# Loads and stores of a per-sample matrix product carry two tiles each instead of one

## The chip, the core and the metric

The kernel runs on one core of a Trainium2 chip; the other cores are idle. The metric is the device time of one launch in microseconds (us). The inputs and the output lie in the chip's memory (HBM), and each of the core's 16 DMA engines moves a share of every transfer between HBM and the on-chip memory (SBUF).

## What is computed

Each of 128 samples has a matrix x of 128 channels by 1024 times, and a subject number from 0 to 7 that picks one of eight 128x128 weight matrices. The product is added to x:

```python
w = weights[subjects]                       # 128 x 128 x 128, picked by subject
out = jnp.einsum('bct,bcd->bdt', x, w)      # per sample
x = x + out                                 # fp32, 128 x 128 x 1024
```

64 MiB (67.1 MB) are read and as many are written, all fp32.

## The kernel before

**Tiles.** One tile is two samples, 1 MiB: 128 partitions with 8 KB each, where the partition holds two neighbouring channels of one sample, side by side. The first 64 partitions are the first sample and the other 64 the second. In HBM a tile is one contiguous 1 MiB. There are 64 tiles, worked in 8 turns of 8. x_ring holds 8 tiles of input, out_ring 8 tiles of output, one slot for each tile of a turn, 64 KB per partition each. Each slot has a semaphore of its own for its load (`x_loaded[s]`) and one for its store (`stored[s]`); a transfer raises its semaphore by 16, one by each DMA engine.

**Set-up.** SyncE's queue issues the load of the weights (0.5 MB, line 71) and then the loads of tiles 0 to 7 (line 73). TensorE (line 123) and VectorE (line 153) build a table in which each weight matrix already contains the identity, so that the addition of x comes with the product. GpSimd (line 112) copies the chosen matrix of each sample from the table to `selected`, four tiles ahead at most.

**Per tile.** TensorE (lines 130 to 145) waits for the tile's load, for its selected weights, and for the PSUM buffer of two tiles earlier, and runs 16 matmuls of 64x512 into `products` (two PSUM buffers); it then counts up `product_ready`. VectorE (line 168) and ScalarE (line 189) each copy half of the products to the tile's slot in out_ring, after `stored[s]` has shown that the slot's store of a turn earlier has landed. ScalarE then waits for both halves and issues the tile's store (line 195).

**Loads of later turns.** SyncE's queue does nothing but this: it waits until `product_ready` shows that tile k is multiplied, and issues the load of tile k + 8 into the same slot (line 80). The loads and the stores therefore form two streams, one issued by SyncE and one by ScalarE, and both are carried out by the same 16 DMA engines.

Of the kernel before, what the change touches and what calls it, by code (L numbers as in the profile page):

```python
# [7 lines left out]
I32 = mybir.dt.int32  # L8

TILES_PER_TURN = 8  # L10
PSUM_BUFS = 2
SELECT_BUFS = 4
BANK = 512
DMA = 16
HALF = 64

DRAINED_FREE = 2 * PSUM_BUFS
PRODUCT_FREE = SELECT_BUFS


def subject_mix_kernel(nc: bass.Bass, x: bass.AP, subjects: bass.AP, weights: bass.AP, out: bass.AP):
    samples, channels, times = x.shape
    n_subjects, _, mixed = weights.shape
    row = 2 * times
    tiles = samples // 2
    turns = tiles // TILES_PER_TURN
    banks = times // BANK
    wide = 2 * mixed
    flat = n_subjects * mixed
    assert channels == mixed == 2 * HALF and banks * BANK == times and flat == times  # L30
    assert turns * TILES_PER_TURN == tiles and TILES_PER_TURN % SELECT_BUFS == 0


    x_rows = x.rearrange("b (q e) t -> (b q) (e t)", e=2)
    out_rows = out.rearrange("b (q e) t -> (b q) (e t)", e=2)

    with ExitStack() as ctx:  # L37
        def sem(name):
            return ctx.enter_context(nc.semaphore(name))

        x_ring = ctx.enter_context(nc.sbuf_tensor("x_ring", [channels, TILES_PER_TURN, row], F32))
        out_ring = ctx.enter_context(nc.sbuf_tensor("out_ring", [channels, TILES_PER_TURN, row], F32))
        loaded = ctx.enter_context(nc.sbuf_tensor("loaded", [channels, n_subjects, mixed], F32))
# [6 lines left out]
        subject_row = ctx.enter_context(nc.sbuf_tensor("subject_row", [1, samples], I32))  # L50
        products = ctx.enter_context(nc.psum_tensor("products", [mixed, PSUM_BUFS, 2, times], F32))

# [5 lines left out]
        weights_spread = sem("weights_spread")  # L58
        table_ready = sem("table_ready")
        weights_selected = sem("weights_selected")  # L60
        x_loaded = [sem(f"x_loaded{s}") for s in range(TILES_PER_TURN)]
        stored = [sem(f"stored{s}") for s in range(TILES_PER_TURN)]
        product_ready = sem("product_ready")
        even_drained = sem("even_drained")
        odd_drained = sem("odd_drained")
# [3 lines left out]
        @block.sync  # L69
        def _(sp):  # L70
            sp.dma_start(loaded[:], weights.rearrange("n c d -> c n d")).then_inc(weights_loaded, DMA)
            for s in range(TILES_PER_TURN):
                sp.dma_start(x_ring[:, s], x_rows[s * channels:(s + 1) * channels, :]).then_inc(x_loaded[s], DMA)

            with sp.Fori(0, turns - 1) as turn:
                for s in range(TILES_PER_TURN):
                    tile = turn * TILES_PER_TURN + s

                    sp.wait_ge(product_ready, PRODUCT_FREE + tile + 1)
                    sp.dma_start(x_ring[:, s], x_rows[bass.ds((tile + TILES_PER_TURN) * channels, channels), :]  # L80
                                 ).then_inc(x_loaded[s], DMA)

        @block.gpsimd
        def _(pool):
# [30 lines left out]
        @block.tensor  # L115
        def _(pe):
            pe.sem_inc(product_ready, PRODUCT_FREE)
            pe.wait_ge(spread_ready, 1)
            pe.wait_ge(weights_loaded, DMA)
            for e in range(2):  # L120
                for n in range(banks):
                    cols = slice(n * BANK, (n + 1) * BANK)
                    last = nc.tensor.matmul(products[:, 0, e, cols], spread[:, e * channels:(e + 1) * channels],  # L123
                                            loaded[:].rearrange("c n d -> c (n d)")[:, cols], start=True, stop=True)
                last.then_inc(weights_spread, 1)

            with pe.Fori(0, turns) as turn:
                for s in range(TILES_PER_TURN):
                    tile = turn * TILES_PER_TURN + s
                    k, b = s % SELECT_BUFS, s % PSUM_BUFS  # L130
                    pe.wait_ge(x_loaded[s], turn * DMA + DMA)
                    pe.wait_ge(weights_selected, 2 * tile + 2)

                    pe.wait_ge(even_drained, DRAINED_FREE + 2 * (tile - PSUM_BUFS) + 2)
                    pe.wait_ge(odd_drained, DRAINED_FREE + 2 * (tile - PSUM_BUFS) + 2)
                    for n in range(banks):
                        for e in range(2):
                            for g in range(2):
                                part = slice(g * HALF, (g + 1) * HALF)
                                last = nc.tensor.matmul(  # L140
                                    products[:, b, g, n * BANK:(n + 1) * BANK],
                                    selected[part, k, e * mixed:(e + 1) * mixed],
                                    x_ring[part, s, e * times + n * BANK:e * times + (n + 1) * BANK],
                                    start=(e == 0), stop=(e == 1))
                    last.then_inc(product_ready, 1)

        @block.vector
        def _(dve):
            dve.sem_inc(even_drained, DRAINED_FREE)
            dve.wait_ge(unit_ready, 2)  # L150
            for e in range(2):
                dve.wait_ge(weights_spread, e + 1)  # L152
                nc.vector.tensor_tensor(  # L153
                    table[:, :, e * mixed:(e + 1) * mixed].rearrange("p n (b m) -> p n m b", b=2),
                    products[:, 0, e, :].rearrange("p (n m b) -> p n m b", n=n_subjects, b=2),
                    unit[:, e * mixed:(e + 1) * mixed].rearrange("p (m b) -> p m b", b=2).unsqueeze(1).to_broadcast(
                        [channels, n_subjects, HALF, 2]),
                    ALU.add).then_inc(table_ready, 1)

            def go_round(turn, first=False):  # L160
                for s in range(TILES_PER_TURN):
                    tile = turn * TILES_PER_TURN + s
                    dve.wait_ge(product_ready, PRODUCT_FREE + tile + 1)
                    if not first:

                        dve.wait_ge(stored[s], turn * DMA)
                    for b in range(2):
                        nc.vector.tensor_copy(out_ring[0:HALF, s, b * times:(b + 1) * times],  # L168
                                              products[b * HALF:(b + 1) * HALF, s % PSUM_BUFS, 0, :]
                                              ).then_inc(even_drained, 1)  # L170

            go_round(0, first=True)
            with dve.Fori(1, turns) as turn:  # L173
                go_round(turn)

        @block.scalar
        def _(act):
            act.dma_start(subject_row[:], subjects.rearrange("(a b) -> a b", a=1)).then_inc(subjects_loaded, DMA)
            act.sem_inc(odd_drained, DRAINED_FREE)

            def go_round(turn, first=False):
                for s in range(TILES_PER_TURN):
                    tile = turn * TILES_PER_TURN + s
                    act.wait_ge(product_ready, PRODUCT_FREE + tile + 1)
                    if not first:

                        act.wait_ge(stored[s], turn * DMA)  # L187
                    for b in range(2):
                        nc.scalar.copy(out_ring[HALF:channels, s, b * times:(b + 1) * times],  # L189
                                       products[b * HALF:(b + 1) * HALF, s % PSUM_BUFS, 1, :]  # L190
                                       ).then_inc(odd_drained, 1)

                    act.wait_ge(odd_drained, DRAINED_FREE + 2 * tile + 2)
                    act.wait_ge(even_drained, DRAINED_FREE + 2 * tile + 2)
                    act.dma_start(out_rows[bass.ds(tile * channels, channels), :],
                                  out_ring[:, s]).then_inc(stored[s], DMA)

            go_round(0, first=True)
            with act.Fori(1, turns) as turn:
                go_round(turn)  # L200
            for s in range(TILES_PER_TURN):
                act.wait_ge(stored[s], turns * DMA)


# [14 lines left out]
```

## Time and profile before

| | us |
|---|---|
| time, median of 3 runs | 327.03 |
| lowest and highest of the 3 | 325.48, 327.35 |
| time of the profiled execution | 326.79 |
| span of that execution, first to last instruction | 324.8 |
| TensorE busy | 239.8 (74%) |
| VectorE busy | 160.2 (49%) |
| ScalarE busy | 130.0 (40%) |
| GpSimd busy | 52.7 (16%) |

The profiled execution stands 0.24 us under the median, and its span 2.0 us under its own time. A DMA is issued by an instruction of a queue (SPq is SyncE's, ACTq is ScalarE's) that lasts a third to half of a microsecond; the movement itself goes on afterwards and is seen in the DMA share, in GB/s, and in the time from issue to landing. The releaser that the profile names for a wait is inferred: where the named engine was done already, it was another, often a DMA.

### The profile page before, as it was taken

To read this page: it belongs to the slowest core of one execution; us is meant where nothing else is said; L and a number is where in the kernel's file an instruction comes from. 1 tells how busy PE (TensorE), PEld (TensorE's weight loads), DVE (VectorE), ACT (ScalarE), POOL (GpSimd) and SP (SyncE) were. 2 spreads that over 40 slices of the span, in tenths; PEclk is the share of its full clock that TensorE was granted. 3 is DMA by queue.
4 is the path that set the end of the run, shared out by engine and by line. 5 is a ranking of instruction groups with operands and counts; after the bars stand their busy time and mean duration, and the time that the engine had idled before them with its cause. 6 is when DMAs were issued, how large, how long until landed. Compare 5 with 4: busy or idle time off the path is not lost.

```text
span 324.8 us, 4203 instructions
## 1 busy us (share of the span) xinstructions
PE 239.8 (74%) x1032; PEld 111.6 (34%) x1032; DVE 160.2 (49%) x130; ACT 130.0 (40%) x129; POOL 52.7 (16%) x137
## 2 busy tenths in 40 slices
PE   3499999999787787786776867768768677687600
PEld 1145555554243343342332332323323333333200
DVE  0437767767546446355354464453544645535410
ACT  1026646556434334334244243342443433424400
POOL 2132122222111111111111011111110111100000
PEclk9979999999999999999999999999999999999955
DMA  7999999999999999999999999999999999999992
GB/s 267 423 422 423 425 427 427 426 426 428 427 428 428 427 427 428 427 428 425 430 424 430 424 428 427 428 427 427 427 428 426 429 426 427 428 426 428 427 428 123
DMA packets 19478, 134.78 MB, mean 415 GB/s; under 512 B 2066, under 2 KB 3091, under 8 KB 3091
## 3 DMA queue, kind: packets, MB, share of 16 engines
q1 hardware_dynamic: 10256, 67.64, 49.7%
q10 hardware_dynamic: 9218, 67.11, 49.0%
q8 instruction: 1, 0.02, 0.0%
q14 instruction: 3, 0.02, 0.0%
HBM read 67.63 MB, written 67.11 MB: 415 GB/s over the span
## 4 chain that ended last, share of the span: by engine, by line
PE 73%; DVE 11%; ACT 5%; issue 2%; DMA 1%; DVEq 1%; POOL 1%; POOLq 1%; ACTq 0%
PE products L140 72%; DVE out_ring L168 10%; ACT out_ring L189 5%; DMA loaded<-weights 1%; DVE table L153 1%; PE products L123 1%; DVEq L37 1%; POOL selected L112 1%; POOLq L107 0%; POOLq L112 0%; ACTq L187 0%; POOLq L101 0%; DVEq L173 0%; POOLq L111 0%; DVEq L152 0%
## 5 line engine op out<-in xcount | busy, mean ns | idle before, releaser
L140 PE MATMUL products<-x_ring,selected 64*128 64x512 f32 x1024 | 234.2, 601 | 61.9 <-DVE out_ring L168 35.0
L168 DVE COPY out_ring<-products 64x1024 f32<-64x1024 f32 x128 | 156.4, 1222 | 140.2 <-PE products L140 138.2
L189 ACT COPY out_ring<-products 64x1024 f32<-64x1024 f32 x128 | 128.7, 1006 | 177.6 <-PE products L140 176.1
L140 PEld LDWEIGHTS products<-x_ring,selected 64*128 64x128 f32 x1024 | 109.3, 188 | 186.7 <-issue 139.3
L112 POOL COPY selected<-table 64x256 f32 x128 | 51.0, 398 | 234.8 <-PE products L140 177.9
L123 PE MATMUL products<-loaded,spread 128*128 128x512 f32 x8 | 5.7, 876 | 5.4 <-DMA loaded<-weights 5.4
L153 DVE TENSOR_TENSOR table<-products,unit 128x1024 f32<-128x1024 f32 x2 | 3.8, 1942 | 9.2 <-PE products L123 9.2
L123 PEld LDWEIGHTS products<-loaded,spread 128*128 128x128 f32 x8 | 2.2, 295 | 8.0 <-issue 8.0
L189 ACT ACT_TABLE_LOAD x1 | 1.3, 1283 | 1.5 <-PEq L210 1.5
L96 POOL TENSOR_SCALAR_AFFINE_SELECT unit<-ones 64x256 f32<-64x256 f32 x2 | 0.8, 404 | 0.1
L88 POOL TENSOR_SCALAR_AFFINE_SELECT spread<-ones 128x256 f32<-128x256 f32 x1 | 0.4, 419 | 0.1
L85 POOL MEMSET ones<- 128x256 f32 x1 | 0.3, 312 | 0.3 <-POOLq L210 0.3
L210 POOL MEMSET const-float32-0.0<- 128x1 f32 x1 | 0.1, 99 | 0.1
L210 POOL MEMSET const-bfloat16-1.0<- 128x1 bf16 x1 | 0.1, 102 | 0.0
L210 POOL MEMSET const-uint8-127<- 128x1 uint8 x1 | 0.1, 102 | 0.0
L210 POOL MEMSET const-float32-1.0<- 128x1 f32 x1 | 0.1, 99 | 0.0
L210 POOL BASE_LOAD x1 | 0.0, 17 | 0.2 <-issue 0.2
## 6 DMA issues: line engine op xcount, KB each, us to landing
x_ring<-x SPq DMA_DIRECT2D x64, 1024.0 KB, 35.0
out<-out_ring ACTq DMA_DIRECT2D x64, 1024.0 KB, 35.5
loaded<-weights SPq DMA_DIRECT2D x1, 512.0 KB, 4.3
subject_row<-subjects ACTq DMA_DIRECT2D x1, 0.5 KB
```

The costliest lines, as they stand in the source:

```text
L37: with ExitStack() as ctx:
L85: nc.gpsimd.memset(ones[:], 1.0).then_inc(ones_ready, 1)
L88: nc.gpsimd.affine_select(spread[:], ones[:], [[-1, 2], [0, 2], [-2, HALF]], ALU.is_equal, 0.0, base=0, channel_multiplier=1).then_inc(spr ...
L96: nc.gpsimd.affine_select(unit[part, :], ones[part, :], [[1, 2], [-1, mixed]], ALU.is_equal, 0.0, base=0, channel_multiplier=2).then_inc(u ...
L112: nc.gpsimd.tensor_copy(selected[part, k:k + 1, :], table[part, bass.ds(subject, 1), :]).then_inc(weights_selected, 1)
L123: last = nc.tensor.matmul(products[:, 0, e, cols], spread[:, e * channels:(e + 1) * channels], loaded[:].rearrange("c n d -> c (n d)")[:, ...
L140: last = nc.tensor.matmul(products[:, b, g, n * BANK:(n + 1) * BANK], selected[part, k, e * mixed:(e + 1) * mixed], x_ring[part, s, e * ti ...
L153: nc.vector.tensor_tensor(table[:, :, e * mixed:(e + 1) * mixed].rearrange("p n (b m) -> p n m b", b=2), products[:, 0, e, :].rearrange("p ...
L168: nc.vector.tensor_copy(out_ring[0:HALF, s, b * times:(b + 1) * times], products[b * HALF:(b + 1) * HALF, s % PSUM_BUFS, 0, :]).then_inc(e ...
L189: nc.scalar.copy(out_ring[HALF:channels, s, b * times:(b + 1) * times], products[b * HALF:(b + 1) * HALF, s % PSUM_BUFS, 1, :]).then_inc(o ...
L210: nc = bacc.Bacc("TRN2", target_bir_lowering=False, num_devices=1)
```

## The change

Loads and stores are issued for two neighbouring tiles at a time (`SPAN = 2`), 2 MiB each. HBM is viewed as partition, tile, 8 KB, so that one transfer takes 8 KB from each of two tiles for every partition. There is one semaphore for two slots of a ring, 4 for each ring in place of 8. The load of tiles k + 8 and k + 9 waits until tiles k and k + 1 are both multiplied; the store of a pair is issued when both tiles are drained. TensorE, VectorE and ScalarE wait for a load or for a free pair of slots only at the first tile of a pair. The sizes of the rings, the matmuls, the copies, the PSUM buffers and GpSimd's part are as before.

```diff
-    x_rows = x.rearrange("b (q e) t -> (b q) (e t)", e=2)
+    x_rows = x.rearrange("b (q e) t -> (b q) (e t)", e=2).rearrange("(t p) f -> p t f", p=channels)
...
-        x_loaded = [sem(f"x_loaded{s}") for s in range(TILES_PER_TURN)]
-        stored = [sem(f"stored{s}") for s in range(TILES_PER_TURN)]
+        x_loaded = [sem(f"x_loaded{s}") for s in range(0, TILES_PER_TURN, SPAN)]
+        stored = [sem(f"stored{s}") for s in range(0, TILES_PER_TURN, SPAN)]
...
-            for s in range(TILES_PER_TURN):
-                sp.dma_start(x_ring[:, s], x_rows[s * channels:(s + 1) * channels, :]).then_inc(x_loaded[s], DMA)
+            for s in range(0, TILES_PER_TURN, SPAN):
+                sp.dma_start(x_ring[:, s:s + SPAN], x_rows[:, s:s + SPAN, :]).then_inc(x_loaded[s // SPAN], DMA)
...
-                    sp.wait_ge(product_ready, PRODUCT_FREE + tile + 1)
-                    sp.dma_start(x_ring[:, s], x_rows[bass.ds((tile + TILES_PER_TURN) * channels, channels), :]
-                                 ).then_inc(x_loaded[s], DMA)
+                    sp.wait_ge(product_ready, PRODUCT_FREE + tile + SPAN)
+                    sp.dma_start(x_ring[:, s:s + SPAN], x_rows[:, bass.ds(tile + TILES_PER_TURN, SPAN), :]
+                                 ).then_inc(x_loaded[s // SPAN], DMA)
...
-                    pe.wait_ge(x_loaded[s], turn * DMA + DMA)
+                    if s % SPAN == 0:
+                        pe.wait_ge(x_loaded[s // SPAN], turn * DMA + DMA)
...
-                    if not first:
-
-                        act.wait_ge(stored[s], turn * DMA)
+                    if not first and s % SPAN == 0:
+
+                        act.wait_ge(stored[s // SPAN], turn * DMA)
...
-                    act.wait_ge(odd_drained, DRAINED_FREE + 2 * tile + 2)
-                    act.wait_ge(even_drained, DRAINED_FREE + 2 * tile + 2)
-                    act.dma_start(out_rows[bass.ds(tile * channels, channels), :],
-                                  out_ring[:, s]).then_inc(stored[s], DMA)
+                    if s % SPAN == SPAN - 1:
+
+                        act.wait_ge(odd_drained, DRAINED_FREE + 2 * tile + 2)
+                        act.wait_ge(even_drained, DRAINED_FREE + 2 * tile + 2)
+                        at = s - SPAN + 1
+                        act.dma_start(out_rows[:, bass.ds(tile - SPAN + 1, SPAN), :],
+                                      out_ring[:, at:s + 1]).then_inc(stored[s // SPAN], DMA)
```

VectorE's wait changes as ScalarE's does, and `out_rows` as `x_rows`. On SyncE's queue, from the first loads into the loop over the later turns, the kernel before has these rows (an ISA row carries the wait; a DMA row's shape is partitions x elements):

```order
1 L71 DMA loaded<-weights 128x8x128
2 L73 DMA x_ring<-x 128x2048 x8
3 L75 UNCONDITIONAL_BRANCH
4 L75 ISA
5 L80 ISA [waits product_ready]
6 L80 DMA x_ring<-x 128x2048
7 L79 REGISTER_ALU
8 L80 ISA [waits product_ready]
9 L80 DMA x_ring<-x 128x2048
```

and the changed kernel these (two lines have moved down in the file):

```order
1 L73 DMA loaded<-weights 128x8x128
2 L75 DMA x_ring<-x 128x2x2048 x4
3 L77 UNCONDITIONAL_BRANCH
4 L77 ISA
5 L82 ISA [waits product_ready]
6 L82 DMA x_ring<-x 128x2x2048
7 L82 ISA [waits product_ready]
8 L82 DMA x_ring<-x 128x2x2048
```

Where one tile's product released one load of a tile, the second product of a pair now releases one load of two. On ScalarE, in the first turn, the kernel before has

```order
3 L189 COPY out_ring<-products 64x1024 [waits product_ready]
4 L189 COPY out_ring<-products 64x1024
5 L195 DMA out<-out_ring 128x2048 [waits even_drained,odd_drained]
6 L189 COPY out_ring<-products 64x1024 [waits product_ready]
7 L189 COPY out_ring<-products 64x1024
8 L195 DMA out<-out_ring 128x2048 [waits even_drained,odd_drained]
```

and the changed one

```order
3 L192 COPY out_ring<-products 64x1024 [waits product_ready]
4 L192 COPY out_ring<-products 64x1024
5 L192 COPY out_ring<-products 64x1024 [waits product_ready]
6 L192 COPY out_ring<-products 64x1024
7 L200 DMA out<-out_ring 128x2x2048 [waits even_drained,odd_drained]
```

The first tile's store, with its wait for VectorE's half, is gone from between the two tiles, and the pair's store stands behind the second.

## Rows read from the trace of the kernel before

**Rows 1.** The page's slices of 8.1 us: DMA busy tenths, GB/s, packets.

```profile
DMA  7999999999999999999999999999999999999992
GB/s 267 423 422 423 425 427 427 426 426 428 427 428 428 427 427 428 427 428 425 430 424 430 424 428 427 428 427 427 427 428 426 429 426 427 428 426 428 427 428 123
DMA packets 19478, 134.78 MB, mean 415 GB/s; under 512 B 2066, under 2 KB 3091, under 8 KB 3091
```

**Rows 2.** Windows: stretch, length, engines' busy us, granted clock, DMA share, GB/s.

```profile
0.00:2.00 2.00, 0.00 (x0) 0.00 (x0) 0.00 (x0) 0.49 (x1) 1.21 (x8) 1.00 0.00 1
2.00:24.00 22.00, 13.95 (x40) 6.45 (x42) 6.23 (x4) 2.80 (x3) 4.53 (x12) 0.92 1.00 403
26.00:318.00 292.00, 223.89 (x986) 104.06 (x982) 152.56 (x125) 125.34 (x125) 46.61 (x117) 0.99 1.01 427
```

**Rows 3.** DMA issues: KB each, median us from issue to landing.

```profile
x_ring<-x SPq DMA_DIRECT2D x64, 1024.0 KB, 35.0
out<-out_ring ACTq DMA_DIRECT2D x64, 1024.0 KB, 35.5
```

**Rows 4.** Chain of the last 30 us: start, duration, what.

```profile
298.38 3.72 PE products L140 x16
...
303.37 3.72 PE products L140 x16
```

**Rows 5.** Line 80 from 267 to 268 us: last load of all.

```profile
L80 SPq DMA_DIRECT2D x_ring<-x x1: 333/333/333, 267.3 to 267.3; - x1
...
DMA to landing us min/median/max: 35.7/35.7/35.7
```

**Rows 6.** Windows of the last 8 us, columns as in rows 2.

```profile
316.00:318.00 2.00, 0.00 (x0) 0.00 (x0) 0.00 (x0) 0.00 (x0) 0.00 (x0) 0.50 0.99 418
318.00:320.00 2.00, 0.00 (x0) 0.00 (x0) 0.00 (x0) 0.00 (x0) 0.00 (x0) 0.50 0.40 168
320.00:322.00 2.00, 0.00 (x0) 0.00 (x0) 0.00 (x0) 0.00 (x0) 0.00 (x0) 0.50 0.07 29
322.00:324.00 2.00, 0.00 (x0) 0.00 (x0) 0.00 (x0) 0.00 (x0) 0.00 (x0) 0.50 0.06 25
```

**Rows 7.** Timeline, 0 to 30 us: start, duration, engine, line, operation, idle before.

```profile
0.87 0.45 SPq L71 DMA_DIRECT2D loaded<-weights  x1
...
21.34 17.48 SPq L80 DMA_DIRECT2D x_ring<-x  x6
...
23.74 0.39 ACTq L195 DMA_DIRECT2D out<-out_ring  x1
...
24.61 2.47 DVE L168 COPY out_ring<-products 64x1024 f32<-64x1024 f32 x2 [0.96 <-PE products L140]
...
27.17 0.34 ACTq L195 DMA_DIRECT2D out<-out_ring  x1
...
28.04 2.47 DVE L168 COPY out_ring<-products 64x1024 f32<-64x1024 f32 x2 [0.96 <-PE products L140]
```

**Rows 8.** Windows at the first transfers, columns as in rows 2.

```profile
1.50:2.00 0.50, 0.00 (x0) 0.00 (x0) 0.00 (x0) 0.49 (x1) 0.43 (x2) 1.00 0.01 2
2.00:2.50 0.50, 0.00 (x0) 0.00 (x0) 0.00 (x0) 0.50 (x1) 0.43 (x2) 1.00 0.71 125
```

**Rows 9.** Line 80 from 24.7 to 24.8 us: the load of tile 9.

```profile
L80 SPq DMA_DIRECT2D x_ring<-x x1: 343/343/343, 24.8 to 24.8; - x1
...
DMA to landing us min/median/max: 9.0/9.0/9.0
```

**Rows 10.** DMA queues: packets, MB, share of 16 engines' span.

```profile
q1 hardware_dynamic: 10256, 67.64, 49.7%
q10 hardware_dynamic: 9218, 67.11, 49.0%
```

**Rows 11.** Line 195 from 309.7 to 310 us: the last store.

```profile
L195 ACTq DMA_DIRECT2D out<-out_ring x1: 338/338/338, 309.8 to 309.8; - x1
...
DMA to landing us min/median/max: 14.5/14.5/14.5
```

More of the change, by code:

```diff
@@ L10 @@
 TILES_PER_TURN = 8
+SPAN = 2
 PSUM_BUFS = 2
@@ L31, in subject_mix_kernel @@
     assert turns * TILES_PER_TURN == tiles and TILES_PER_TURN % SELECT_BUFS == 0
-    x_rows = x.rearrange("b (q e) t -> (b q) (e t)", e=2)
-    out_rows = out.rearrange("b (q e) t -> (b q) (e t)", e=2)
+    x_rows = x.rearrange("b (q e) t -> (b q) (e t)", e=2).rearrange("(t p) f -> p t f", p=channels)
+    out_rows = out.rearrange("b (q e) t -> (b q) (e t)", e=2).rearrange("(t p) f -> p t f", p=channels)
     with ExitStack() as ctx:
@@ L71, in _ @@
             sp.dma_start(loaded[:], weights.rearrange("n c d -> c n d")).then_inc(weights_loaded, DMA)
-            for s in range(TILES_PER_TURN):
-                sp.dma_start(x_ring[:, s], x_rows[s * channels:(s + 1) * channels, :]).then_inc(x_loaded[s], DMA)
+            for s in range(0, TILES_PER_TURN, SPAN):
+                sp.dma_start(x_ring[:, s:s + SPAN], x_rows[:, s:s + SPAN, :]).then_inc(x_loaded[s // SPAN], DMA)
             with sp.Fori(0, turns - 1) as turn:
-                for s in range(TILES_PER_TURN):
+                for s in range(0, TILES_PER_TURN, SPAN):
                     tile = turn * TILES_PER_TURN + s
-                    sp.wait_ge(product_ready, PRODUCT_FREE + tile + 1)
-                    sp.dma_start(x_ring[:, s], x_rows[bass.ds((tile + TILES_PER_TURN) * channels, channels), :]
-                                 ).then_inc(x_loaded[s], DMA)
+                    sp.wait_ge(product_ready, PRODUCT_FREE + tile + SPAN)
+                    sp.dma_start(x_ring[:, s:s + SPAN], x_rows[:, bass.ds(tile + TILES_PER_TURN, SPAN), :]
+                                 ).then_inc(x_loaded[s // SPAN], DMA)
         @block.gpsimd
@@ L163, in go_round @@
                     dve.wait_ge(product_ready, PRODUCT_FREE + tile + 1)
-                    if not first:
-                        dve.wait_ge(stored[s], turn * DMA)
+                    if not first and s % SPAN == 0:
+                        dve.wait_ge(stored[s // SPAN], turn * DMA)
                     for b in range(2):
@@ L184, in go_round @@
                     act.wait_ge(product_ready, PRODUCT_FREE + tile + 1)
-                    if not first:
-                        act.wait_ge(stored[s], turn * DMA)
+                    if not first and s % SPAN == 0:
+                        act.wait_ge(stored[s // SPAN], turn * DMA)
                     for b in range(2):
@@ L200, in _ @@
                 go_round(turn)
-            for s in range(TILES_PER_TURN):
-                act.wait_ge(stored[s], turns * DMA)
+            for s in range(0, TILES_PER_TURN, SPAN):
+                act.wait_ge(stored[s // SPAN], turns * DMA)
 def kernel(x, itok_B_0_7, L0_cond_weights):
```

## The prediction

> **What bounds the kernel now.** I read the slices of the page first. The DMA engines are busy in 9 tenths or more of every slice but the first and the last, at 422 to 430 GB/s [rows 1], while TensorE is busy for 74% and no other engine for half. The windows say it more sharply: from 26 to 318 us the DMA share is 1.01 and the rate 427 GB/s [rows 2]. The 134.78 MB at 427 GB/s are 315.6 us, of a span of 324.8. So only 9.2 us of the span aren't paid for in bytes: some 2 us before the first byte, a lower rate on the way to 24 us (403 GB/s over 22 us, 1.2 us), and the end.
>
> The second view is the issues: a load lands 35.0 us after its issue and a store 35.5 [rows 3]. The tiles at the end start 4.99 us apart on TensorE though 16 matmuls take 3.72 [rows 4]. Landing time over cadence, (35.0 + 35.5) / 4.99, is 14.1 tiles in flight of the 16 that the rings hold. TensorE is waiting for loads: the last load, issued at 267.3, lands 35.7 us later, at 303.0 [rows 5], and TensorE starts tile 63 at 303.37 [rows 4]. That the profile names VectorE as releaser there is a coincidence.
>
> The third view is the last 8 us. The DMA share falls from 0.99 to 0.40, and then stays at 0.07 and 0.06 up to 324 [rows 6]. One engine of 16 is 0.0625. So 15 engines are done at about 318.8 (0.40 x 2 us after 318), and one goes on alone for some 5.1 us. Each engine has the same share of every transfer, so this one is slower by 5.1 of 320, 1.6%. It never lacks work, and the end of the kernel is its end. What counts for the change is therefore how long this slow engine is without work, and how much work it has.
>
> **The change, part by part.**
>
> *The bytes and the 8 KB runs* stay as they are: 134.2 MB, 315 us. Nothing is gained there unless the rate goes up.
>
> *The first refill comes later.* This is the one place where the queue of loads runs dry. The first eight loads and the weights are 8 x 1.0486 + 0.52 = 8.91 MB. By 24.0 us 403 x 22 = 8.87 MB have moved [rows 2], so at the granted rate the engines are through with them at 24.1. Before, tile 0's product releases a load issued at 21.34 [rows 7], early enough that the rate doesn't dip. Now the pair's load waits for tile 1's product. VectorE starts on that at 24.61 [rows 7], and the load of tile 9 which it released was issued at 24.76; that is when the load of tiles 8 and 9 is issued now. No store can fill in: before, the first was issued at 23.74, now tiles 0 and 1 go together at 27.17 [rows 7]. From the issue to the first byte on idle engines: the weights were issued at 0.87, and nothing moves up to 2.0 (share 0.01 from 1.5 to 2.0, then 0.71) [rows 8], so 1.1 us. First bytes at 24.76 + 1.1 = 25.9: a gap of 1.8 us for the mean engine. The slow engine gets less of it, since it finishes the first loads later; by how much I can only bound, by nothing and by 1.6% of the 22 us, 0.35 us. I take **+1.5 us**. For the upper bound of the launch itself there is the load of tile 9, 9.0 us from issue to landing [rows 9]: sharing the engines evenly with a store it needs 2 x 2.46 = 4.9 us of transfer, which leaves 4.1 us. That row has other work in front of it, and the weights' row has idle engines as here, so I go by 1.1; the bounds of the gap are 1.4 and 4.8 us.
>
> After that the engines stay covered: 2 tiles of loads (4.9 us, to 30.8), a pair of stores issued at 27.17 and moving by 28.3 to 31.3 (another 4.9, to 35.7 at least), and the next pair of loads released by tile 3's product at 28.04 + 3.43 = 31.5. TensorE has its tiles until well past there: by 28 us it has multiplied three of the eight that lie in the ring since 24.1 or so.
>
> *The steady state.* A load is issued up to one tile later (4.99 us), and a store too. The price is zero as long as something else lies in the queues. With pairs, the rings keep at most two loaded tiles at TensorE and two more not yet reloaded, and as many on the store side: of 16 tiles at least 12 remain in flight by the same count that gives 14.1 now. Twelve tiles are 29 us of work. If that cover were gone, each turn would lose up to 5 us, 40 in all; it is far from gone.
>
> *Half of the semaphore writes.* 2,048 of the packets under 512 B (of 2,066) [rows 1] are the 16 increments of each of 128 transfers; 1,024 stay, 64 fewer per engine. The trace gives a bound on their cost: the queue of loads has 1,038 small packets more than that of stores (the weights' among them) and 0.7% more of 16 x 324.8 us, 36.4 us, so 35 ns per small packet [rows 10]. 64 x 35 ns = 2.2 us at most; the least is zero. These packets carry 4 B, those of the weights 512 B, which at 26.7 GB/s an engine are 19 ns by themselves, and the difference holds the slower first reads too. I take 8 ns, **-0.5 us**.
>
> *Fewer issues.* SyncE's queue issues 32 transfers for 64, ScalarE 32 for 64, each 0.33 us [rows 5, 11]. Both queues spend most of their time waiting for products of a TensorE that waits for loads, so this is worth nothing; nor are fewer waits. If it were on the path it would be 32 x 0.34 = 11 us, but no wait ends with it.
>
> *The end.* The last pair's store is issued when tile 63 is drained, and carries tile 62 too. Now the last store is issued at 309.8 and lands 14.5 us later [rows 11], of which it needs 1.1 to launch and 2.5 to move; some 10.5 us it lies behind older stores on the slow engine. With pairs, TensorE may start tile 62 only when 63 is there too, so one more tile of 3.7 us lies between the last load and the last product, and the last store is 2.5 us longer: 10.5 - 6.2 = 4.3 us of cover are left. Price 0; beyond 4.3 us of further delay the end moves one for one.
>
> Sum, against the profiled execution: 326.79 + 1.5 - 0.5 = **327.8 us**. It stood 0.24 us below the median of 327.03, within their spread of 1.9 us.
>
> The Trainium skill, "Perfetto Trace Analysis", section "DMA Optimizations", says against this change that splitting transfers may let some start sooner. By that rule joining them is late only where engines lie idle, which is the gap at 24 us and the same sum. The skill's "DMA: Bandwidth & Descriptors", section "Anatomy of one DMA", gives a fixed cost of about 2.0 us a transfer; if it stood in series, 64 transfers fewer would save 128 us (an estimate from that page). The trace has 9.2 us outside its bytes, so here that cost is hidden by the other transfers in flight.
>
> **The rivals.**
>
> *The launch is slow (slower).* If the 2 MB load needs the 4.1 us of the upper bound and not 1.1, the gap is 1.5 + 3.0 = 4.5 us: 326.8 + 4.5 - 0.5 = 330.8. For it speaks the row of tile 9 and that twice the descriptors must be made; against it that this row's engines had other work. It decides over my forecast from a launch of 3.6 us on, where the time passes 330.3.
>
> *The slow engine loses its lag (faster).* If what holds back one engine goes with the order of the addresses or the number of transfers, and vanishes, all finish together: 327.8 - 5.1 = 322.7. If only half goes, 325.2. For it: the lag is the largest single item beyond the bytes. Against it: nothing in the change is aimed at one engine, and each still gets the same partitions.
>
> *The gap stays out.* If the engines have more left at 24 us than I think or the launch is overlapped, 326.8 - 0.5 = 326.3.
>
> *The rate falls (slower).* One engine now reads 8 KB runs in turn from two places 1 MiB apart. The rows of before have no such pattern. Each 1% of rate is 3.2 us; a fall to 422 GB/s gives 327.8 + 3.7 = 331.5. The Trainium skill, "DMA: Bandwidth & Descriptors", section "Latency and other measured facts", has copies whose rows lie 512 KiB apart 3% below the full rate, and 2 MiB apart 23% below. No run here shows that; neighbouring partitions stay 8 KB apart in this change, and only the two halves of a pair are 1 MiB apart.
>
> *The end is uncovered (slower).* If the loads end over 4.3 us later among the stores than now, the last pair is late; at 8 us that makes 331.5.
>
> **How the numbers follow.** My forecast 0.60, slow launch 0.13, lag gone 0.10, gap absent 0.10, rate 0.04, end 0.03. A measurement here can tell about 1% from no change, 323.8 to 330.3 us. The forecast and the absent gap lie inside that; of the lag's 0.10 I count 0.08 as over 1%; of the slow launch 0.09 is over 330.3, with 0.06 of the last two. Faster 0.08, within 1% 0.77, slower 0.15. The range must leave out no more than 2 in 10: from 325.0 (the absent gap with the spread of the runs) to 331.0 (the slow launch included) it leaves out 0.08 to 0.10 below and 0.07 above.
>
> **What would show it.** Right: windows at 24 to 26 us with a DMA share near 0.2 to 0.5, and the full 427 GB/s from 28 us to some 320; TensorE's tiles in pairs, two back to back (3.4 to 3.7 us each) and then a wait, 9.9 us a pair; landing times of loads and stores still 30 us and more; one engine alone for about 5 us at the end. Wrong: no dip at 24 us; a dip of more than 4 us; a rate other than 427 in the middle; a second dip near 31 us or before 318; or an end at which all 16 engines stop together.

## The result, and the profile after

The changed kernel takes 329.46 us (median of 4 runs, 328.5 to 330.53) against 327.0 for the kernel before: a ratio of 1.0079, 95% interval 1.0047 to 1.0111, or 2.5 us more. The forecast was 327.8 us with a range of 325.0 to 331.0: the time lies in the range and the change has the forecast's sign, but it is 1.7 us more than forecast. A second set of 9 runs gave 329.41 and 1.0082 (1.0048 to 1.0115). In the experiments below, a few executions fell in a slower state of the chip (361 us and more); they are left out of the ratios and of the medians given here. The profiled execution took 328.5 us, with a span of 326.4. VectorE, ScalarE and GpSimd are as busy as before.

The slices of the changed kernel's page, DMA busy tenths, GB/s and packets, answer to [rows 1]:

```profile
DMA  7998999999999999999999999999999999999994
GB/s 264 423 406 280 426 430 426 427 429 428 427 430 425 428 431 426 428 429 426 429 427 428 429 427 427 431 426 428 429 426 429 430 426 427 428 427 430 428 414 194
DMA packets 18453, 134.78 MB, mean 413 GB/s; under 512 B 1041, under 2 KB 2066, under 8 KB 2066
```

Only the third and the fourth slice are clearly lower, 406 and 280 GB/s. The windows of the changed kernel from 22 us on (columns as in [rows 2]; the last two are DMA share and GB/s):

```profile
22.00:24.00 2.00, 2.00 (x12) 0.96 (x10) 1.31 (x2) 0.90 (x1) 0.16 (x1) 1.00 1.00 414
24.00:26.00 2.00, 2.00 (x12) 1.02 (x10) 1.67 (x2) 1.68 (x2) 0.79 (x2) 1.00 0.30 78
26.00:28.00 2.00, 2.00 (x12) 0.88 (x11) 1.04 (x2) 0.60 (x2) 0.14 (x1) 1.00 0.95 324
28.00:30.00 2.00, 2.00 (x12) 0.97 (x10) 1.97 (x2) 1.74 (x2) 0.65 (x2) 1.00 1.05 373
30.00:32.00 2.00, 2.00 (x12) 1.01 (x10) 1.04 (x2) 0.84 (x1) 0.39 (x1) 1.00 0.98 291
32.00:34.00 2.00, 2.00 (x12) 0.88 (x11) 1.61 (x2) 1.17 (x2) 0.40 (x1) 1.00 0.99 414
40.00:300.00 260.00, 210.79 (x882) 99.62 (x880) 133.86 (x111) 110.09 (x111) 42.76 (x108) 0.93 1.01 428
```

The dip at 24 us is there, where the forecast put it. But it has two parts. In the first two microseconds the engines have nothing to do most of the time (share 0.30): (427 - 78) x 2 / 427 = 1.6 us. Then, for 8 us, the engines count as busy (0.95 to 1.05) and yet move only 291 to 414 GB/s: (103 + 54 + 136 + 13) x 2 / 427 = 1.4 us. Together 3.1 us. From 40 to 300 us the rate is 428 GB/s. By queue (packets, MB, share of the engines; q1 are the loads, q10 the stores), from 24 to 33 us nearly all that moves are loads:

```profile
q1 hardware_dynamic: 282, 2.17, 74.1%
q10 hardware_dynamic: 46, 0.38, 9.9%
```

and in the steady state, from 100 to 300 us:

```profile
q10 hardware_dynamic: 5555, 42.88, 50.7%
q1 hardware_dynamic: 5538, 42.63, 50.4%
```

These rows say which packets are slow. From 24 to 33 us the loads take 0.741 x 16 x 9 = 107 us of engine time for 2.17 MB, 49 us a MB, and the stores 38 us a MB; in the steady state both take 38. So the few stores move as fast as ever, and the loads take 1.3 times as long.

The timeline of the changed kernel's queues around the dip, which answers to [rows 7]:

```profile
24.44 7.24 SPq L82 DMA_DIRECT2D x_ring<-x  x2
...
26.86 0.43 ACTq L200 DMA_DIRECT2D out<-out_ring  x1
```

The load of tiles 8 and 9 is issued at 24.44, when the engines are nearly through with the first eight. The DMA share from 24 to 33 us in 40 slices of 0.225 us (tenths, each packet counted where it starts):

```profile
DMA  5300009029691969999899979999691989897999
```

Next to nothing starts from 24.45 to 25.35. Packet by packet, the new load starts at 25.47 with eight packets at once, and the next follow from 26.02 on. So the launch, from the issue to the first packet, took 1.0 us, not 4.1.

The chain of waits near the end, with start, duration and what, answers to [rows 4]:

```profile
274.55 7.15 PE products L143 x32
...
284.51 8.85 PE products L143 x32
...
294.42 7.15 PE products L143 x32
...
304.36 8.85 PE products L143 x32
```

TensorE works in pairs of tiles, 9.9 us apart; before, one tile followed another after 4.99 us. The last windows answer to [rows 6]:

```profile
316.00:318.00 2.00, 0.00 (x0) 0.00 (x0) 0.00 (x0) 0.00 (x0) 0.00 (x0) 0.50 0.86 360
318.00:320.00 2.00, 0.00 (x0) 0.00 (x0) 0.00 (x0) 0.00 (x0) 0.00 (x0) 0.50 1.03 426
320.00:322.00 2.00, 0.00 (x0) 0.00 (x0) 0.00 (x0) 0.00 (x0) 0.00 (x0) 0.50 0.90 373
322.00:324.00 2.00, 0.00 (x0) 0.00 (x0) 0.00 (x0) 0.00 (x0) 0.00 (x0) 0.50 0.09 37
```

The mean engine is done at about 321.8 and one goes on alone to some 325.2. The share of 0.86 from 316 to 318 is new: the faster engines ran out of stores before the last pair's, issued at 315.9, was there. The slow engine didn't: the pair before, issued at 304.3, landed with its last engine 16.7 us later, at 321.0.

### The profile page after: what moved, and what is told of

Same layout as the page of the kernel before. It is cut to its first block, busy times and chain, and to the rows that moved or that the text cites. A ratio compares the mean times of both kernels' runs of the same rounds, so it can differ in the third digit from the quotient of the medians.

```text
span 326.4 us, 3895 instructions
## 1 busy us (share of the span) xinstructions
PE 251.0 (77%) x1032; PEld 118.1 (36%) x1032; DVE 160.0 (49%) x130; ACT 129.9 (40%) x129; POOL 52.4 (16%) x137
## 4 chain that ended last, share of the span: by engine, by line
PE 59%; DMA 19%; DVE 8%; issue 8%; ACT 2%; DVEq 1%; POOLq 0%; POOL 0%; ACTq 0%
PE products L143 58%; DMA out<-out_ring 18%; DVE out_ring L171 7%; ACT out_ring L192 2%; DMA loaded<-weights 1%; DVE table L156 1%; PE products L125 1%; DVEq L39 1%; POOLq L109 0%; POOL selected L114 0%; DVEq L176 0%; POOLq L114 0%; POOLq L103 0%; ACTq L200 0%; POOLq L113 0%
## 5 line engine op out<-in xcount | busy, mean ns | idle before, releaser
L143 PE MATMUL products<-x_ring,selected 64*128 64x512 f32 x1024 | 245.7, 635 | 56.9 <-DVE out_ring L171 36.8
L143 PEld LDWEIGHTS products<-x_ring,selected 64*128 64x128 f32 x1024 | 116.0, 201 | 186.6 <-issue 135.7
## 6 DMA issues: line engine op xcount, KB each, us to landing
x_ring<-x SPq DMA_DIRECT2D x32, 2048.0 KB, 30.5
out<-out_ring ACTq DMA_DIRECT2D x32, 2048.0 KB, 32.2
```

What stands on the lines that cost most here:

```text
L143: last = nc.tensor.matmul(products[:, b, g, n * BANK:(n + 1) * BANK], selected[part, k, e * mixed:(e + 1) * mixed], x_ring[part, s, e * ti ...
```

## The experiments

All ratios are against the kernel before, run on the same chip.

**Late release, or larger transfers?** Transfers of one tile as before, but released in pairs:

```diff
-                    sp.wait_ge(product_ready, PRODUCT_FREE + tile + 1)
+                    if s % 2 == 0:
+                        sp.wait_ge(product_ready, PRODUCT_FREE + tile + 2)
...
-                    act.dma_start(out_rows[bass.ds(tile * channels, channels), :],
-                                  out_ring[:, s]).then_inc(stored[s], DMA)
+                    if s % 2 == 1:
+                        act.wait_ge(odd_drained, DRAINED_FREE + 2 * tile + 2)
+                        act.wait_ge(even_drained, DRAINED_FREE + 2 * tile + 2)
+                        for one in (s - 1, s):
+                            act.dma_start(out_rows[bass.ds((tile - s + one) * channels, channels), :],
+                                          out_ring[:, one]).then_inc(stored[one], DMA)
```

> Transfers stay at one tile each (128 of them, one semaphore each), but loads 8 and 9, 10 and 11 and so on are released together by the second product of a pair, and the stores of a pair are issued together once both tiles are drained. Theory A (the loss comes from the late release: the load queue runs dry at 24 us): the same dip as in the changed kernel, DMA share near 0.3 from 24 to 26 us, the rate under 400 GB/s until 32 us, some 3 us lost, and no gain from fewer semaphores: 329 to 331 us. Theory B (the loss comes from 2 MB transfers that read from two places 1 MiB apart): the dip lasts 1.5 us only and the rate is back at 420 from 26 us on: 328 to 328.5 us.

Measured: 329.68 us, 1.0095 (1.0063 to 1.0126). Its windows:

```profile
24.00:26.00 2.00, 2.00 (x12) 1.11 (x10) 1.26 (x2) 1.27 (x2) 0.79 (x2) 1.00 0.40 78
26.00:28.00 2.00, 2.00 (x12) 0.97 (x10) 1.18 (x1) 0.74 (x1) 0.00 (x1) 1.00 0.68 287
28.00:30.00 2.00, 2.00 (x12) 1.02 (x10) 1.83 (x2) 1.79 (x2) 0.79 (x2) 1.00 1.00 385
30.00:32.00 2.00, 2.00 (x12) 1.11 (x10) 1.04 (x2) 0.64 (x2) 0.29 (x1) 1.00 0.94 274
```

The same dip with the same second part, without a single transfer of 2 MB. The late release alone gives a loss as large as the change does (1.0095 against 1.0079 and 1.0082). Of the size of the transfers and of the alternation between two places in HBM no share is seen; the intervals would hide one of 1 us or so. The slow part after the gap isn't due to the 2 MB transfers.

**The first pair released singly.** In the changed kernel, slots 0 and 1 are loaded by two transfers, each after its own product (in the first turn too), on the pair's semaphore with waits for twice 16:

```diff
+                    if s == 0:
+                        for one in range(SPAN):
+                            sp.wait_ge(product_ready, PRODUCT_FREE + tile + one + 1)
+                            sp.dma_start(x_ring[:, one:one + 1], x_rows[:, bass.ds(tile + one + TILES_PER_TURN, 1), :]
+                                         ).then_inc(x_loaded[0], DMA)
+                        continue
```

> The changed kernel, but the first pair of each turn is loaded as two transfers of one tile, each released by its own product, both on the pair's semaphore with a wait for the sum. Theory A: tile 0's product releases a load at 21 us again, no dip at 24 us, and the 3 us of the dip come back, while the smaller number of semaphore writes stays: 325.0 to 326.5 us, under the kernel before. Theory B: the 2 MB transfers go on costing something; 328 us and more.

Measured: 327.37 us, 1.0003 (0.9976 to 1.0029). With the loads alone mended, the ratio of 1.0079 has become 1.0003. It doesn't get under the kernel before, where 325.0 to 326.5 us had been expected. Its trace has two places with less than the full rate. From 34 to 38 us, where again nearly nothing but loads moves, the rate is 385 and 319 GB/s; and near the end the engines run out of work, since the last pair's store is issued only at 315.07:

```profile
36.00:38.00 2.00, 2.00 (x12) 1.06 (x10) 1.50 (x2) 1.07 (x2) 0.38 (x1) 1.00 0.94 319
...
314.00:316.00 2.00, 0.00 (x0) 0.00 (x0) 0.85 (x1) 0.41 (x1) 0.00 (x0) 1.00 0.34 143
```

The first pair's stores treated in the same way:

> The changed kernel with the first pair of each turn loaded and stored as single tiles; the other three pairs of a turn as pairs. Theory A (both streams have nothing to do at 24 us because load and store of the first pair come late): no dip is left, and the fewer semaphore writes show: 325.5 to 326.8 us, below the kernel before by 0.1 to 0.5%. Theory B (pairs cost something in the steady state): 327.5 us and more.

Measured: 326.48 us, 0.9992 (0.9965 to 1.0019), no difference from the kernel before that can be told.

```profile
36.00:38.00 2.00, 2.00 (x12) 1.08 (x10) 1.48 (x2) 1.05 (x2) 0.39 (x1) 1.00 0.93 291
...
314.00:316.00 2.00, 0.00 (x0) 0.00 (x0) 0.00 (x0) 0.00 (x0) 0.00 (x0) 0.50 1.01 426
```

The slow loads at 36 us are still there, though theory A had no dip left; what is gone in this trace is the hole near the end (the last store is issued at 311.96). The two kernels' intervals overlap.

**One direction at a time.** Loads of two tiles with stores of one, and the reverse:

> Only the loads carry two tiles; stores carry one, issued as each tile is drained. Theory A: the load is late as in the changed kernel, but the first store is issued at 23.7 and fills in from 25 or 26 us; the dip is shorter, 1 to 2 us lost, with half of the saving by fewer semaphores: 327 to 328.5 us. Theory B: as the changed kernel, 329 to 330 us.

> Only the stores carry two tiles; loads carry one. Theory A: the first refill is released at 21.3 us as before, so no dip at 24 us, but with the first store issued at 27 us the load of tile 9 (issued at 24.8) stands alone and may leave a small one near 27 us; half of the saving by fewer semaphores: 326 to 327.5 us. Theory B: the stores' part of the loss shows, 328 us or more.

Measured: loads only 327.70 us, 1.0024 (0.9991 to 1.0058); stores only 326.87 us, 0.9983 (0.9956 to 1.0011). The one costs perhaps 0.8 us, which its interval can't tell from nothing, and the other nothing; together they cost 2.5. The queues run dry only if both are late: with loads late, tile 0's store fills in. The windows of the kernel with loads only show it, 0.85 where the changed kernel has 0.30:

```profile
24.00:26.00 2.00, 2.00 (x12) 1.04 (x10) 1.38 (x2) 1.39 (x2) 0.39 (x1) 1.00 0.85 348
26.00:28.00 2.00, 2.00 (x12) 1.10 (x10) 1.06 (x1) 0.62 (x1) 0.40 (x1) 1.00 0.96 274
```

Here too the share is near 1 while the rate is 274. The kernel with stores only did have a dip in its trace (274, 324 and 344 GB/s from 24 to 30 us, with loads alone and a share of 0.83 to 0.99), which theory A had not expected: in that execution its first refill was issued at 23.18 us, not 21.3, because TensorE's first tile was slow (granted clock 0.50, 0.50 and 0.55 from 16 to 22 us, where the kernel before had 0.56, 0.58 and 1.00). Near the end it too ran out of work (share 0.38 from 316 to 318 us). Its median shows neither. The late refill led to the next two.

**The clock of the first tile.** A second trace of each kernel, unchanged:

> The changed kernel, unchanged. If the dip belongs to the kernel, the second trace shows the same four windows from 24 to 32 us (near 78, 324, 373 and 291 GB/s); if the slow reads from 26 to 32 us are chance, these differ widely. Time 328.5 to 330.5 us.

> The kernel before, unchanged, for a second trace on another execution. If the lag of the slow DMA engine is a fixed property, the last 5 us show one engine of 16 alone again, and the full rate at 24 to 34 us; if it is chance, its length differs by a microsecond or more.

Measured: the changed kernel's second profiled execution took 330.46 us, 2.0 more than the first. Windows of that second execution:

```profile
14.00:16.00 2.00, 0.03 (x2) 0.06 (x2) 0.00 (x0) 0.00 (x0) 0.79 (x2) 0.50 0.99 414
...
18.00:20.00 2.00, 2.00 (x8) 0.91 (x6) 0.00 (x0) 0.00 (x0) 0.92 (x3) 0.50 1.00 418
...
24.00:26.00 2.00, 2.00 (x12) 0.92 (x10) 1.04 (x2) 0.61 (x1) 0.40 (x1) 1.00 0.01 4
26.00:28.00 2.00, 2.00 (x12) 1.02 (x10) 1.84 (x2) 1.40 (x2) 0.40 (x1) 1.00 0.74 152
```

In the first execution the granted clock was 0.85, 0.50 and 0.79 in the windows from 14 to 20 us, here 0.50 in all three. TensorE works at 1.2 GHz for longer, the load of tiles 8 and 9 is issued at 25.54 for 24.44, and the gap is wider by that much (share 0.01, then 0.74). The slow part comes again as well: 418, 283 and 344 GB/s from 28 to 34 us. Both parts together are (423 + 275 + 9 + 144 + 83) x 2 / 427 = 4.4 us, for 3.1 in the first execution. So the dip belongs to the kernel, and its length moves with the clock of the first tile. The kernel before is shielded from that by issuing at 21.34, 2.8 us before the engines run dry. Its second execution took 325.33 us against 326.79, with the full rate around 24 us. The lone engine's part at its end was shorter:

```profile
318.00:320.00 2.00, 0.00 (x0) 0.00 (x0) 0.00 (x0) 0.00 (x0) 0.00 (x0) 0.50 0.39 164
320.00:322.00 2.00, 0.00 (x0) 0.00 (x0) 0.00 (x0) 0.00 (x0) 0.00 (x0) 0.50 0.08 33
322.00:324.00 2.00, 0.00 (x0) 0.00 (x0) 0.00 (x0) 0.00 (x0) 0.00 (x0) 0.50 0.01 4
```

The other 15 stop at 318.8 as in [rows 6], the last at about 322.3, not 324: the lag is 3.5 us here and 5.1 there, in the same kernel.

Then the clock was changed on purpose, by five matmuls in the idle time ahead of the first tile:

```diff
                 last.then_inc(weights_spread, 1)
+            for _ in range(5):
+                nc.tensor.matmul(products[:, 1, 0, 0:BANK], spread[:, 0:channels],
+                                 loaded[:].rearrange("c n d -> c (n d)")[:, 0:BANK], start=True, stop=True)
```

> The changed kernel plus five matmuls (128x512, into the PSUM buffer that tile 1 will overwrite) on TensorE between the table and the first tile, where it is idle from 10.6 to 15.5 us and its granted clock then falls to 0.50. Nothing else changes. Theory A (the loss is the time between the last first-turn load and tile 1's product): if the clock stays at 1.00, tile 0 takes 3.7 us for 5.4 and tile 1's product comes near 22.7 us for 24.3 to 25.4; its load is issued 1.0 us before the queue is dry at 24.1, so the dip at 24 us nearly vanishes, and with half of the semaphore writes the time is 326.0 to 327.2 us. If the clock matters nothing or pairs themselves cost, 329 us as before.

> The same five matmuls added to the kernel before. Its first refill is issued at 21.3 us, 1.7 us ahead of need, so a faster first tile gives nothing: 326.5 to 327.3 us. If the clock at the start were worth time by itself, it would be 325 us or less.

Measured: the changed kernel with them 328.13 us, 1.0036 (1.0014 to 1.0059); the kernel before with them 325.74 us, 0.9979 (0.9954 to 1.0005). The changed kernel's windows with them:

```profile
18.00:20.00 2.00, 2.00 (x12) 1.08 (x10) 0.51 (x1) 0.51 (x1) 0.79 (x2) 1.00 1.00 418
...
24.00:26.00 2.00, 2.00 (x12) 1.09 (x10) 1.37 (x2) 0.96 (x1) 0.22 (x1) 1.00 0.81 221
26.00:28.00 2.00, 2.00 (x12) 1.05 (x10) 1.61 (x2) 1.62 (x2) 0.79 (x2) 1.00 1.10 348
28.00:30.00 2.00, 2.00 (x12) 0.97 (x11) 1.04 (x2) 0.60 (x2) 0.08 (x1) 1.00 0.86 246
30.00:32.00 2.00, 2.00 (x12) 1.10 (x10) 1.97 (x2) 1.80 (x2) 0.71 (x2) 1.00 1.00 381
```

The clock stays at 1.00 and the load is issued at 23.07. The gap has nearly gone (0.81 for 0.30), and the ratio has come down from 1.0082 to 1.0036. Not all of these 1.5 us need be the gap's: the kernel before, which has no gap, came out at 0.9979 with the same matmuls, under the 326.5 to 327.3 expected, though its interval just includes no change. The second part stays: 221 to 381 GB/s from 24 to 32 us are (206 + 79 + 181 + 46) x 2 / 427 = 2.4 us. My expectation of 326.0 to 327.2 missed this: it held that only the empty time costs. With a load queue one transfer deep and no store moving yet, the engines are busy and the loads are slow. What slows them stays open. One transfer ahead in the queue isn't enough by itself to bring it on: the kernel before has just that from 24 to 26 us, no store moving, and goes at 422 GB/s.

**What a transfer costs.** Half tiles, 64 partitions each, 256 transfers:

```diff
-                    sp.dma_start(x_ring[:, s], x_rows[bass.ds((tile + TILES_PER_TURN) * channels, channels), :]
-                                 ).then_inc(x_loaded[s], DMA)
+                    for h in range(2):
+                        sp.dma_start(x_ring[h:channels:2, s], x_halves[bass.ds((tile + TILES_PER_TURN) * HALF, HALF), h, :]
+                                     ).then_inc(x_loaded[s], DMA)
```

> The kernel before with each tile moved by two transfers of half its partitions (64 even, 64 odd), 8 KB runs as before, 256 transfers and 4,096 semaphore writes for 2,048, all released as before. It prices one transfer more. If a semaphore write costs what I took, 8 ns on each engine, 128 more per engine are 1 us: 328 us. If it costs the bound of 35 ns, 4.5 us: 331.5 us. If nothing, 327 us. The half number in the changed kernel then gave back half of what is seen here.

Measured: 328.20 us, 1.0052 (1.0023 to 1.0082), 1.7 us more for 128 more transfers, so 13 ns each (21 by the upper end of the interval). Even that is more than the transfers' own price, because its trace has a slow stretch too: 381, 393, 406, 291 and 295 GB/s from 24 to 34 us are (46 + 34 + 21 + 136 + 132) x 2 / 427 = 1.7 us, as much as the whole difference. The run therefore gives no price of a transfer, only a bound. From 40 to 300 us it moves 426 GB/s, the kernel before 427 and the changed one 428 (427 in its second trace): one part in 427 is 0.7 us over the kernel.

**Four tiles at a time.** `SPAN = 4`, nothing else:

> SPAN = 4: each load and store carries four tiles, released by the fourth product. Theory A by its own count: the refill waits for tile 3's product, at 24.3 + 2 x 3.43 = 31.2 us, so the gap is 32.2 - 24.1 = 8 us; the end is uncovered too, since after the last load 4 tiles have to be multiplied (14 us) and a store of 10 us follows, 27 us against some 20 us of older stores. 326.8 + 8 + 6 - 1.3 = 339 us, between 334 and 346. If only the number of transfers counted, 325.5 us.

Measured: 344.54 us, 1.0563 (1.0508 to 1.0617). Windows at the first refill and at the end:

```profile
24.00:32.00 8.00, 8.00 (x40) 3.90 (x38) 5.92 (x5) 4.62 (x5) 1.58 (x4) 1.00 0.02 8
...
324.00:326.00 2.00, 2.00 (x12) 0.97 (x11) 1.97 (x2) 1.60 (x2) 0.00 (x0) 1.00 0.00 0
326.00:330.00 4.00, 0.99 (x6) 0.16 (x2) 2.51 (x3) 2.01 (x2) 0.00 (x0) 1.00 0.00 0
```

The gap is 10 us, to 34, since in this execution the load was issued at 33.0; and some 7 us before 330 the engines are empty once more, while the last four tiles are worked. With the same two rings, coarser transfers first lose the start and then the end.

**Both remedies together.** The first pair singly in both directions, and the five matmuls:

> The two remedies together: the first pair of each turn loaded and stored as single tiles, the other pairs as pairs, and the five matmuls that keep TensorE's clock up before the first tile. 80 transfers for each direction's 128 in all, the load of tile 8 issued near 19 us. If the dip is the whole loss of the change and a transfer costs some 13 ns per engine (from the run with half tiles), 0.6 us stay as the gain: 325.5 to 326.5 us. If pairs cost something in the steady state or the warm start is worth nothing, 326.5 to 327.5 us.

Measured: 325.86 us, 0.9978 (0.9959 to 0.9996), 0.2% under the kernel before; from 24 to 32 us it moves 397 to 438 GB/s. Against the kernel before with the matmuls alone (0.9979) it shows no gain, so pairs as such are worth nothing that can be measured here.

## Why the prediction was right, and where it was off

**What bounds the kernel.** Right. TensorE was busy 11 us longer in the changed kernel (251.0 us), its clock 0.92 for 0.97 on the mean, and it cost nothing between 40 and 300 us: 428 GB/s.

**The first refill.** The right place, and the experiments show the mechanism: with it undone the loss is gone, and with it alone (transfers of one tile) the loss is there. The size was off. The prediction had 1.5 us for the gap, and the gap was that: 1.6 us of empty engines. The windows give 3.1 us in all, and the other 1.4 are of busy engines at a low rate. The step that failed is "after that the engines stay covered": they were, and covered engines were taken to run at 427 GB/s. The prediction had asked for the full rate from 28 us on and named a second dip near 31 us as a sign that it is wrong; from 30 to 32 us the rate was 291 GB/s. The launch was 1.0 us, as the predicted 1.1, so the rival with 4.1 us falls. It is this rival that had carried the range up to 331.0; that the time of 329.46 lies inside is to that extent luck. The prediction also took tile 1's product at a fixed 24.6 us; it moves by a microsecond with the granted clock.

**The first rival's row.** The 9.0 us of [rows 9] were a load that shared the engines, as the prediction said.

**Half of the semaphore writes.** -0.5 us was predicted, and no run shows it. The rates of 426, 427 and 428 GB/s for 256, 128 and 64 transfers would agree with it, but the second trace of the changed kernel has 427 and `SPAN = 4` has 424. The half tiles bound it: 64 x 13 ns = 0.85 us, or 1.3 us by the upper end of the interval.

**The steady state.** Free, as predicted. Loads land 30.5 us after issue and stores 32.2, for 35.0 and 35.5 [rows 3]; that is (30.5 + 32.2) / 4.97 = 12.6 tiles in flight, where at least 12 were predicted.

**The rate.** The rival with a lower rate from the alternation between two places falls with 428 GB/s.

**The fixed cost of a transfer.** The 2.0 us that the prediction takes from the Trainium skill are given there for transfers that GpSimd issues, not for those of SyncE and ScalarE, which this kernel has. The prediction's sum didn't use them.

**The end.** The last store was issued at 315.9 and landed 10.0 us later, of which it needs 1.1 + 5.0. So 3.9 us of cover were left to the slow engine, 4.3 predicted. (By the prediction's own rows it should have been 4.7: 14.5 - 1.1 - 2.5 is 10.9, not 10.5.) The faster engines had none (0.86), which costs nothing as long as the slow one ends last. How near this is to costing something is seen in the kernel with the first pair's loads single and in the one with stores only, where the share falls to 0.34 and 0.38 in two microseconds near the end.

**The slow engine.** That its lag sets the end is right. That it lies in the kernel is not: it was 5.1 and 3.5 us in two executions of the kernel before. In the profiled pair it probably hid part of the loss: 326.79 + 3.1 - 0.5 would be 329.4, and the execution took 328.5, with a lone engine from 321.8 to some 325.2, 3.4 us. The median of 329.46 agrees with the sum, but the 3.1 are of one execution, and another had 4.4.

## What to carry to other kernels

Where the DMA engines are full, as here, the size of a transfer between 0.5 and 2 MB was worth next to nothing (426 to 428 GB/s), and what it moved was the moment at which the next one might be issued. Look for the one place where a queue is short, most often where the first slots of a ring are refilled, and take the distance from the releasing product to the moment the queue is dry: here it went from 2.8 us ahead to 0.3 behind, and 0.9 or 1.0 us ahead (stores only, and the changed kernel with the matmuls) was not enough for the full rate. Keep the first refills fine and release them singly, and let a short queue of loads be backed by stores.

## What had not been expected

- While the queues were being filled anew, the engines were counted busy (mostly 0.86 to 1.10) and moved only 221 to 385 GB/s for 4 to 8 us; in steady state the same share moves 427. In the changed kernel's trace it is the loads' packets that take longer, not the stores'; in that of the kernel with loads only the stores' do so too, 55 us a MB for 38 from 26 to 32 us. Nine of the twelve kernels show it between 24 and 40 us, with transfers of half a tile, one, two and four tiles. A gap isn't needed for it: the two kernels with the first pair released singly run at 406 to 434 GB/s from 24 to 34 us and then fall to 319 and 291. Nor is a late issue: the kernel before with the five matmuls has its first refill at 19.14 us, 5 us ahead, and still 360 GB/s from 24 to 26 us. The cause wasn't found.
- With pairs, TensorE waited up to 2.8 us between two of them, and its clock fell again and again: 8.85 us for a pair at times (granted clock 0.50 from 306 to 308 us), 7.15 otherwise. Here it is hidden behind the DMA engines; what it would cost elsewhere no run shows.
- One DMA engine of 16 ended later than the others by 3.4 to 5.1 us in the traces of the kernel before and in the first of the changed kernel, by an amount that differs between executions. Between the two of the kernel before it is 1.6 us, half a per cent.
- From the start of an issue to its first packet on idle engines it took 1.0 us in the changed kernel and 1.1 for the weights. The Trainium skill, "DMA: Bandwidth & Descriptors", section "Latency and other measured facts", gives some 0.6 us to the first byte for such queues. The traces agree with it if one counts from the end of the issuing instruction, which lasts 0.38 and 0.45 us; counted from its start, they have 0.4 to 0.5 us more than that.
